# Linear attention with a mixture of experts on one core: states and state reads in 64x32 tiles, two states in one visit

## The reference

```python
q, k = silu(x @ Wq), silu(x @ Wk); v = x @ Wv          # 16 heads
q, k = lrpe(q, theta), lrpe(k, theta)                  # 8 -> 16 features
energy = einsum('bhnd,bhmd->bhnm', q, k) * tril
out = einsum('bhnm,bhmd->bhnd', energy, v) @ Wo
out = layernorm(out * sigmoid(x @ G1 @ G2)) * gamma + beta
x = layernorm(x + out)
x = layernorm(x + silu(x @ sg) * (x @ su) @ sd + routed(x))
```

## Time and profile before

| | |
|---|---|
| median of 3 runs | 850.86 us (846.95 to 853.42) |
| span of the profiled execution, its own time | 865.4 us |
| PE busy | 817.6 us, 94% |
| DVE busy | 612.6 us, 71% |
| ACT busy | 354.2 us, 41% |
| POOL busy | 397.9 us, 46% |
| mean granted clock of PE | 0.985 |

### The profile page before, as it was taken

One profiled execution on the slowest core, in us unless ns is written; L12 is line 12 of the kernel. 1 busy time (PEld: TensorE's weight loads), 2 busy tenths in 40 slices (PEclk: granted clock), 3 DMA queues, 4 the chain that ended last, 5 costly groups with the idle time before them and its releaser, 6 DMA issues.

```text
span 865.4 us, 27880 instructions
## 1 busy us (share of the span) xinstructions
PE 817.6 (94%) x11178; PEld 665.6 (77%) x11178; DVE 612.6 (71%) x1946; ACT 354.2 (41%) x742; POOL 397.9 (46%) x373
## 2 busy tenths in 40 slices
PE   5889999999999999999998999988999999999995
PEld 4667777677777777777776776677999999999884
DVE  6688887979788797978887787853454444444585
ACT  6334453444445453544433332222333333223575
POOL 6441233322414332341424445545388877776433
PEclk9999999999999999999999999999999999999998
DMA  5235111202111111211121221212255555433455
GB/s 146 45 105 206 41 46 42 51 26 51 47 43 42 46 43 39 51 42 37 47 67 37 65 48 46 64 50 63 83 96 99 99 96 95 63 51 43 108 150 150
DMA packets 74095, 59.89 MB, mean 69 GB/s; under 512 B 10163, under 2 KB 63722, under 8 KB 73968
## 3 DMA queue, kind: packets, MB, share of 16 engines
q1 hardware_dynamic: 56944, 41.84, 17.4%
q0 software_dynamic: 17024, 16.28, 10.5%
HBM read 23.99 MB, written 28.89 MB: 61 GB/s over the span
## 4 chain that ended last, share of the span: by engine, by line
PE 77%; DVE 10%; issue 7%; ACT 2%; DMA 2%; POOL 2%; another core or an unknown queue 0%; DVEq 0%; POOLq 0%; ACTq 0%; SPq 0%
PE bank L1733 6%; PE energy_banks L1794 6%; PE bank L1735 5%; PE bank L1734 5%; PE energy_and_gate_banks L1733 5%; PE bank L1839 4%; PE energy_and_gate_banks L1819 4%; PE bank L2261 4%; PE energy_and_gate_banks L2261 4%; PE energy_and_gate_banks L1735 3%; PE energy_and_gate_banks L1734 3%; PE energy_banks L1733 3%; PE energy_banks L1735 3%; PE energy_banks L1734 3%; PE energy_banks L1787 2%
## 5 line engine op out<-in xcount | busy, mean ns | idle before, releaser
L578 POOL DMA_INDIRECT dispatched_rows<-x,slot x128 | 131.4, 1027 | 211.5 <-PE energy_banks L1794 108.2
L689 POOL DMA_INDIRECT summed_rows<-VP,goal_i x80 | 123.9, 1548 | 43.0 <-issue 22.6
L1020 ACT ACTIVATE sq<-energy_banks 128x512 f32<-128x512 f32 (+1 forms) x96 | 50.6, 527 | 120.0 <-PE energy_banks L1735 112.2
L1168 DVE TENSOR_TENSOR sf<-sf,bank 128x512 f32<-128x512 f32 x88 | 60.4, 687 | 43.7 <-PE bank L1735 41.6
L653 POOL TENSOR_TENSOR rr<-vq,minus_half 128x8 f32<-128x8 f32 x16 | 26.7, 1668 | 105.7 <-DVE vq L1238 105.7
L761 ACT ACTIVATE hidden_rounded<-sf 128x512 fp32r<-128x512 f32 x88 | 55.5, 630 | 35.1 <-DVE sf L1168 23.0
L751 ACT ACTIVATE sf<-energy_and_gate_banks 128x512 f32<-128x512 f32 x88 | 52.7, 599 | 34.7 <-PE energy_and_gate_banks L1735 28.7
L1794 PE MATMUL energy_banks<-EM,VP 64*32 64x64 f32 x4096 | 62.6, 226 | 2.4 <-issue 2.4
L1138 DVE TENSOR_TENSOR EM<-energy_and_gate_banks,causal 128x512 f32<-128x512 f32 x64 | 44.1, 689 | 26.8 <-PE energy_banks L1819 21.6
L1839 PEld LDWEIGHTS bank<-VP,Kt 64*64 64x64 f32 x896 | 35.7, 134 | 30.5 <-issue 19.8
L1839 PE MATMUL bank<-VP,Kt 64*64 64x64 f32 x896 | 51.8, 232 | 6.6 <-DVE SM L1147 3.9
(11 more groups left out here) (246 smaller groups left out, 2269.0 us busy)
## 6 DMA issues: line engine op xcount, KB each, us to landing
QM<-QT SPq DMA_DIRECT2D x248, 32.0 KB
dispatched_rows<-empty POOLq DMA_DIRECT2D x8, 655.0 KB, 6.1
QM<-dispatched_rows SPq DMA_DIRECT2D x8, 655.0 KB
xin<-in_x SPq DMA_DIRECT2D x16, 256.0 KB, 2.9
QM<-summed_rows SPq DMA_DIRECT2D x16, 256.0 KB, 2.9
out_x<-QM SPq DMA_DIRECT2D x16, 256.0 KB, 3.2
summed_rows<-empty SPq DMA_DIRECT2D x13, 256.0 KB
dispatched_rows<-x,slot POOLq DMA_INDIRECT x128
```

The lines of the kernel that those rows point to most:

```text
L578: g.indirect_dma_start(out=xg_d, out_offset=bass.IndirectOffsetOnAxis(ap=slot[:, n % 2, j:j + 1], axis=0), in_=x1[:, n % 2, j % NC, :], in ...
L689: g.indirect_dma_start(out=sum_d, out_offset=bass.IndirectOffsetOnAxis(ap=goal_i[:, par, t:t + 1], axis=0), in_=ye[:, par, t, :], in_offse ...
L1168: v.tensor_tensor(sf[:, n % SF], sf[:, n % SF], UB[:], ALU.mult).then_inc(v_h, 1)
```

## The change

**Tiles.** The state is computed in 64x32 tiles: eight matmuls instead of four, each with 32 of the key features and only the four heads of the same half, so `SBK`, `SM` and `headmask` are 64 columns wide instead of 128 (DVE's `mask_state` handles 64 columns). The read of the state by q, now `from_states`, is in 64x32 tiles too: up to eight matmuls of 64 rows instead of four of 128. Energies by values were in 64x32 tiles before. Half of the reads are "crossed": they take state rows of one half of the array and add to sums that `attend` will later write from the other half of it. They go first, and `attend` waits on a new semaphore `pe_sm` of PE's own until they are done.

**Visits.** `states_and_out(c)` for c > 0 is now: state k = 2c - 1, `from_states` and `attend` for chunk c - 1, state k = 2c. The energies stand alone.

**Orders.** In `with_feed_forward` the parts between are reordered on PE, ACT and DVE; POOL's dispatches wait on other semaphores (energies instead of states). In the other three orders PE's and ACT's parts keep their places but for the states and one `down_back`.

```diff
-        headmask = sb("headmask", [P, 2, 64])
+        headmask = sb("headmask", [P, 2, 32])
...
-                    v.tensor_tensor(SM[:, k], SBK[:, 0:128], headmask[:].rearrange("p t n -> p (t n)"),
+                    v.tensor_tensor(SM[:, k, 0:64], SBK[:, 0:64], headmask[:].rearrange("p t n -> p (t n)"),
...
+            def from_states(b, par, c):
+
+                need(pe, a_out, 4 * b + c)
+                need(pe, v_mask, 8 * b + 2 * c + 2)
+                need(pe, v_S, NS * b + 2 * c + 1)
+                cols = slice(T * c, T * (c + 1))
+                for crossed in (1, 0):
+                    for s in (0, 1):
+                        k, j = 2 * c + s, (s + crossed) % 2
+                        rows = slice(T * j, T * j + T)
+                        for half in (0, 1):
+                            if k > 0:
+                                o = T * half + 32 * j
+                                ins = t.matmul(AV2[o:o + 32, s, cols], SM[rows, k - 1, 32 * half:32 * half + 32],
+                                               QT[rows, par, c // 2, half, P * (c % 2) + T * s:P * (c % 2) + T * (s + 1)],
+                                               start=True, stop=False)
+                    if crossed:
+                        ins.then_inc(pe_sm, 1)
+
             def attend(b, par, c):
 
-                need(pe, a_out, 4 * b + c)
-                need(pe, v_S, NS * b + 2 * c + 1)
-                need(pe, v_mask, 8 * b + 2 * c + 2)
+                need(pe, pe_sm, 4 * b + c + 1)
...
-                        for j in (0, 1):
-                            ins = t.matmul(SBK[64 * j:64 * j + 64, T * half:T * half + T],
-                                           Kt[tok, par, c, P * half + 64 * j:P * half + 64 * j + 64],
-                                           v_rows(par, c, half, tok), start=(k == 0 and half == 0), stop=True,
+                        for j in range(4):
+                            ins = t.matmul(SBK[32 * j:32 * j + 32, 32 * half:32 * half + 32],
+                                           Kt[tok, par, c, P * half + 32 * j:P * half + 32 * j + 32],
+                                           v_rows(par, c, half, j // 2, tok), start=(k == 0 and half == 0), stop=True,
...
-                    if core:
+                    if c == 0:
+                        state(0, 0)
+                        if back:
+                            from_states(b - 1, 1 - par, 3)
+                            attend(b - 1, 1 - par, 3)
+                    else:
+                        state(c - 1, 1)
+                        from_states(b, par, c - 1)
+                        attend(b, par, c - 1)
                         state(c, 0)
```

202 lines of the change are left out of this document (93 added, 109 removed).

## The result

The changed kernel takes 867.05 us (median of 4 runs, 865.00 to 869.66), the kernel before, run beside it, 850.89 us: a ratio of 1.019 with a 95% interval of 1.015 to 1.023. It is slower, by 16 us. The profiled execution took 869.66 us with a span of 867.9.

The account below looks back on a forecast made before the run. PE bounds a feed-forward block's first half; in the second PE and DVE are both full. Span 865.4 + 8.3 (ten blocks) - 3 (six others) = 870.7, as a median 856 us; range 831 to 872, the forecast's own 847 to 868.

Parts of the forecast that it names:

- The likeliest case: Feed-forward blocks +8.3 us, the six others -3, since DVE's order eats PE's savings: 856 us; chance 0.42.
- The visit: State, read, attend, state on PE: 1.62 to 1.67 us, taken as 1.67, from 1.93; the first visit about 1.45.
- self-wait: `attend` waits on PE for the crossed reads to end: 0.33 to 0.37 us instead of 0.23, +0.14 a visit.
- First half: Feed-forward block up to the visit to chunk 2, PE's half: sum -0.83 us, taken as -0.75.
- Second half: Feed-forward block from visit 2: DVE's chain makes gates 3 and 6 wait; 20.65 us instead of 19.07, +1.58.
- The block: One feed-forward block: -0.75 + 1.58 = +0.83 us, ten make +8.3; blocks of 39.1 us would prove the sum.
- The six other blocks: PE loses up to 1.4 us of work each, DVE's order hardly changes: -0.5 a block, so -3.
- its new pacing of the dispatches costs nothing: POOL's dispatches, last now after energies 3, still some 5 us ahead of the rows' reuse: no cost.
- 0.983 of the span, so 856.: Profiled span forecast of 870.7 us turned into a median by the shown ratio, 850.86 being 0.983 of its span.
- PE as the bound throughout: Rival: all PE savings count, 24.5 us off the span, median 827; gates 3 and 6 start without a wait; 0.24.
- The waits did not cancel: Rival: DVE's two idle times (1.75 us a block) shrink, blocks stay at 38.2 us, time 850; chance 0.22.
- The supply of records: Rival: small-tile records held up by their supply, visits 2.13 us, +27 on the forecast's span, 883; chance 0.12.

Follow-up runs that it names:

- norm first: Changed kernel with DVE's gated norm and turn 1 ahead of the copy of piece 3, logits copy ahead of piece 4's: 862.12 us, ratio 1.014.
- filled idle time: Changed kernel, DVE reordered: top-two search and choices ahead of copies 5 and 6, product 6 right behind the addition: ratio 1.000; 0.997 with last four blocks' old visits.
- tiles alone: Kernel before with only the 64x32 tiles for state and read and the wait on crossed reads, old visits and orders: 847.05 us against 850.35, ratio 0.995.
- after: The changed kernel, nothing further edited, against the kernel before: 867.05 us, ratio 1.019; run again, ratio 1.021.
- before again: Kernel before, unchanged, profiled once more for an execution at its usual time: ratio 1.000.
- both gates: Changed kernel, DVE reordered: norm first, and product 5 and chunk 3's masks ahead of centring and addition: 867.31 us, ratio 1.021.
- late visits as before: Changed kernel with the old visits and old GpSimd waits in the last four blocks, 64x32 tiles kept: 859.03 us, ratio 1.011.
- positions early: Changed kernel with DVE's idle time filled and the last blocks' old visits, plus position reads ahead of the second moments: 846.16 us against 849.67, ratio 0.9954.

## Why the prediction was right or wrong

It gave 856 us, 831 to 872, with 0.44 for within 1% and 0.32 for slower; measured were 867.05 and a ratio of 1.019. The range holds it; the forecast's own range, 847 to 868, holds it at its edge (the bounds that it names add up to 844 to 870). The likeliest case had the mechanism in the blocks and nearly its size, and missed most of the loss, which lies outside them.

- **The visit.** 1.45 us instead of 1.67. The self-wait was a little over its price of 0.33 to 0.37: from the reads to the `attend` 303.65 - 303.25 = 0.40. The 16 records of a state take 0.14, not the 0.23 of eight in two tiles: more records over four tiles were not free but cheaper. The first visit is 1.35 against 1.45.
- **First half.** 18.16 us; 19.17 - 0.75 = 18.42 was forecast, and the visits explain the rest. No energies waited for a silu.
- **Second half.** DVE idle 1.68 ahead of the copy of piece 3 (over 1 was said), 1.04 and 0.37 at pieces 5 and 6 (1.3 and 0.45), gate 3 late by about 0.7 (0.87), gate 6 by 319.80 - 318.01 = 1.8 (1.8; the turned keys start at 317.07 and take 0.94 where nothing waits behind them). The half lasted 20.17 against 20.65, shorter by 0.48, as the two visits in it. That these waits are the order of DVE's instructions is shown: norm first gave 0.6 a block back, norm first and the filled idle time together 1.4 (on another chip).
- **The block.** 38.33 us, not 39.1. As a difference the sum was near; the level was off, since the execution read was slow itself. In the one at its usual time the same block is 316.89 - 279.30 = 37.59 us, with halves of 19.13 and 18.46:

```profile
279.30 0.45 PE L1839 MATMUL bank<-VP,Kt 64*64 64x64 f32 x8
298.43 0.45 PE L1839 MATMUL bank<-VP,Kt 64*64 64x64 f32 x8
316.89 0.45 PE L1839 MATMUL bank<-VP,Kt 64*64 64x64 f32 x8
```

So the first half gave -0.97 (-0.75 was forecast), the second +1.71 (+1.58), the block +0.74 (+0.83).
- **The six other blocks** were the step that failed: "DVE's order hardly changes", -3. DVE's order does not change there, but PE's does: reads follow energies at once, and the masks are in between. The last four blocks alone lost 9.1 us against a like execution. All but 1.6 of it came back with the old visits and the old pacing of GpSimd, and as much in two runs in which GpSimd's addition did not meet the turn. So "its new pacing of the dispatches costs nothing" failed with it. How the loss is shared between the waits, the addition and the lower clock is not shown.
- **"0.983 of the span, so 856."** The span forecast, 870.7, lies 0.3% above the 867.9 measured, and that is chance: two errors nearly cancel. The execution read was 17.4 us slower than a like one (1.5, 5.3, 8.3 and 2.3 in the table's four parts), and the change was forecast as 8.3 - 3 = +5.3 us where it was +17.6. The factor took the first error out again: 850.86 + 0.983 x 5.3 = 856. What is left, 11 us, is the change's alone. The execution shown ahead reads like those of chip 3; what slows the kernel before there (stops of 0.6 to 0.7 us from start to start in late attends, as in the earlier trace rows, not tied to packets) stays open.

Of the rivals, PE as the bound throughout is out: gates 3 and 6 wait. The waits did not cancel. The supply of records was real, but not as priced: attends run at 0.64 to 0.8 us, not slower each, and five stops of 1.5 to 2.5 us make about 9 us instead of 27, as many as with the tiles alone. The start floor of the Trainium skill (TensorE: Matmul & The Clock Gate, Back-to-back issue gap) is not seen for tiles side by side here either: 60 records of `attend` start in 304.23 - 303.65 = 0.58 us, 10 ns apart, and the 112 of a visit took 1.45 us.

What the change gains, the tiles alone have (0.5%). The merged visits and the reordered blocks saved PE some 0.6 us of work a block more (35.7 against 36.3, estimated from 293.75 of 299 us busy with the tiles alone), and brought some 2 us of waits: for DVE's masks in the blocks, and for the masks again, with a lower clock, in the last four.

## What to carry to other kernels

When two engines both fill a stretch, work taken off one is won only as far as the other's order lets it: find the instructions that it queues behind a wait which the change moves, and fill that idle time in the same edit. A single profiled execution can be 2% slow: forecast the change as a difference, add it to the usual time, and judge it between like executions, part by part; a total can come near because two errors cancel. Merging steps of many small instructions also shortens the time in which their producers can keep up: look at what comes right before the merged step in every kind of block, not only in the commonest.

## What the runs showed of the hardware

- PE can outrun the supply of its program: it stops for 1.3 to 2.9 us (from one matmul's start to the next's) and goes on 1.2 to 1.5 us after a 16 KB packet of it has landed, in every run here with a stop over 1.2 us that no semaphore explains. Moving the program by 128 instructions moves the stops. The kernels with 12,522 matmul records have four to six stops of over 1 us in stage one, the kernel before with 11,178 none, and one when its program was shifted.
- Such a packet takes 0.9 to 2.0 us, and at these stops it is on its way 2.1 to 2.9 us before PE goes on.
- DVE's turn of 0.68 us took 1.99 and 2.46 with GpSimd's addition of 1.29 beside it, and ended 0.56 us after the addition both times.
- The granted clock from 437 to 500 us was 0.92 in after and in the tiles alone, both with stops there, and 0.97 in before again: after a stop matmuls of 512 columns start 0.43 us apart instead of 0.23 for a while, the lower of the two levels (1.2 of 2.4 GHz). A wait of 2.3 us in each block brought such a drop in seven of eight blocks (both gates) and cost 0.5 to 1.1 us each; the waits of 0.56 and 1.64 us in the changed kernel's blocks brought none there (clock 1.00), and with the late visits as before the clock from 437 to 500 us was 0.97 in spite of two stops. What share of the loss in the last four blocks this is was not separated.
- One chip of four ran the kernel before 2% slower than the others. The idle-filled versions, whose blocks took 36.9 us there, lost in the last four blocks instead (108.3 and 105.4 us, against 94.3 with the positions early on another chip).
